# Last stage: GpSimd folds eight expert products to four only, TensorE sums four products and the tokens

## What is computed

```python
router_probs = softmax(x @ router_w + router_b)
top_p, top_i = top_k(router_probs, 2)
top_p = top_p / sum(top_p)
expert_out = einsum('bnd,edc->bnec', x, expert_w) + expert_b
return einsum('bnk,bnkc->bnc', top_p, take_along_axis(expert_out, top_i))
```

## Time and profile before

| what | us |
|---|---|
| median of 3 runs | 2697.78 |
| lowest and highest run | 2696.98, 2702.96 |
| the profiled execution, its own time | 2704.11 |
| its span in the profile | 2702.3 |
| PE, DVE, ACT, POOL busy in the span | 2410.5, 2324.5, 1593.5, 408.6 |

### The profile page before, as it was taken

One profiled execution on the slowest core, in us unless ns is written; L12 is line 12 of the kernel. 1 busy time (PEld: TensorE's weight loads), 2 busy tenths in 40 slices (PEclk: granted clock), 3 DMA queues, 4 the chain that ended last, 5 costly groups with the idle time before them and its releaser, 6 DMA issues. The chain is left out here.

```text
span 2702.3 us, 46968 instructions
## 1 busy us (share of the span) xinstructions
PE 2410.5 (89%) x18454; PEld 973.5 (36%) x18454; DVE 2324.5 (86%) x4150; ACT 1593.5 (59%) x2090; POOL 408.6 (15%) x456
## 2 busy tenths in 40 slices
PE   3878888369999999999999999999999998898886
PEld 1343333112222222222222222222222224787875
DVE  4577776689999999999999999999999992889997
ACT  1243343427777777777777777777777775343333
POOL 0021111300000000100000000000000000466666
PEclk9989899659999999999999999999999998667777
DMA  7696684320202222012022022021020001132231
GB/s 171 162 250 202 198 253 139 142 78 1 61 1 61 53 75 61 27 35 61 1 61 60 1 61 61 1 60 40 22 61 4 22 25 54 67 108 86 95 108 24
DMA packets 68110, 206.29 MB, mean 76 GB/s; under 512 B 20630, under 2 KB 33554, under 8 KB 61234
## 3 DMA queue, kind: packets, MB, share of 16 engines
q1 hardware_dynamic: 64034, 185.27, 24.7%
q0 software_dynamic: 3040, 15.57, 1.5%
q10 hardware_dynamic: 816, 2.46, 0.3%
HBM read 80.14 MB, written 61.31 MB: 52 GB/s over the span
## 5 line engine op out<-in xcount | busy, mean ns | idle before, releaser
L1331 DVE TENSOR_REDUCE at_XM<-at_psX 128x1 f32<-128x448 f32 x2688 | 1546.1, 620 | 92.0 <-PE at_psX L1182 71.2
L1248 ACT ACTIVATE at_PR<-at_psS 128x896 f32<-128x896 f32 x1344 | 1163.1, 915 | 454.4 <-PE at_psS L1158 452.4
L1200 PE MATMUL at_psV<-at_PR,at_V 128*32 128x448 f32 x5376 | 645.2, 552 | 0.1
L1158 PE MATMUL at_psS<-at_US,at_KS 128*128 128x448 f16 x2688 | 637.0, 357 | 0.7 <-ACT at_PR L1248 0.2
L1182 PE MATMUL at_psX<-at_KS,at_US 64*128 64x448 f16 x1344 | 490.5, 365 | 65.0 <-DVE at_XM L1331 42.7
L1182 PE MATMUL at_psX<-at_KS,at_UH 64*128 64x448 f16 x1344 | 490.5, 365 | 0.0
L1182 PEld LDWEIGHTS at_psX<-at_KS,at_US 64*128 64x128 f16 x1344 | 124.6, 93 | 721.5 <-DVE at_XM L1331 662.0
L1158 PEld LDWEIGHTS at_psS<-at_US,at_KS 128*128 128x128 f16 x2688 | 200.9, 98 | 273.8 <-ACT at_PR L1248 117.1
L1297 POOL CAST at_mrow<-at_mt 7x128 f16<-7x128 f32 x64 | 18.0, 281 | 1612.9 <-DVE at_mt L1350 1260.1
L1602 POOL TENSOR_TENSOR fi_WE<-fi_WE 128x256 f32<-128x256 f32 (+1 forms) x224 | 214.8, 984 | 101.5 <-DVE fi_WE L1656 101.1
L1465 PE MATMUL fi_psO<-fi_wv,fi_SUMS 128*128 128x33 f32 x800 | 153.0, 364 | 6.4 <-PEq L951 6.4
(11 more groups left out here) (199 smaller groups left out, 2010.0 us busy)
## 6 DMA issues: line engine op xcount, KB each, us to landing
sums<-at_O SPq DMA_DIRECT2D x16, 1568.0 KB, 6.3
fi_SUMS<-sums SPq DMA_DIRECT2D x16, 1568.0 KB, 6.8
sb_stacks<-sb_T SPq DMA_DIRECT2D x64, 270.5 KB, 7.3
sb_stacks<-sb_Xp SPq DMA_DIRECT2D x64, 248.8 KB, 10.2
sb_stacks<-sb_Xp SPq DMA_DIRECT2D x64, 248.0 KB, 5.9
sb_stacks<-sb_T SPq DMA_DIRECT2D x64, 172.5 KB, 11.4
at_KS<-key_stacks SPq DMA_DIRECT2D x32, 208.0 KB, 6.8
fi_RES<-residual SPq DMA_DIRECT2D x16, 400.0 KB, 7.2
```

The costliest lines, as they stand in the source:

```text
L1158: last = nc.tensor.matmul(psS[:, at % 2, k, 0:TILE], KS[:, b, (2 * c + k) * P:(2 * c + k + 1) * P], US[:, b, t * TILE:(t + 1) * TILE], sta ...
L1200: last = nc.tensor.matmul(psV[C * q:C * q + C, 0:TILE], V[:, b, G * k + q, :], PR[:, (n * 2 * STEPS + 2 * q4 + q // 2) % PRS, q % 2, :], s ...
L1248: nc.scalar.activation(PR[:, f % PRS], psS[:, at % 2, :, 0:TILE], ACT.Exp).then_inc(p_ready, 1)
L1331: nc.vector.tensor_reduce(o, psX[:, (at + j) % 3, 0:TILE], AX.X, ALU.max).then_inc(x_done, 1)
```

## The change

GpSimd makes only the first fold of each set, from eight products to four, and signals `folded` after it; the second fold, and the wait on its own first one, are gone. TensorE adds four products and the tokens per set, five products instead of three.

```diff
 def sums(n, c):
-                    for e in range(E // 4 + 1):
-                        v = (WE[:, s, e] if e < E // 4 else T1[:, c, G * s:G * s + w // C]).rearrange("p q c -> p (q c)")
+                    for e in range(E // 2 + 1):
+                        v = (WE[:, s, e] if e < E // 2 else T1[:, c, G * s:G * s + w // C]).rearrange("p q c -> p (q c)")
                         last = nc.tensor.matmul(psB[0:w, s // 4, s % 4 * P:(s % 4 + 1) * P], v[:, 0:w], ident[:],
-                                                start=(e == 0), stop=(e == E // 4))
+                                                start=(e == 0), stop=(e == E // 2))
                     last.then_inc(set_done, 1)
...
                 if n > 0:
-                    for s in range(QSETS + 1):
-                        if s < QSETS:
-                            pool.wait_ge(we_ready, n * NU - NU + min(2 * s + 2, NU))
-                            fold(s, E // 2).then_inc(half_folded, 1)
-                        if s >= 1:
-                            pool.wait_ge(half_folded, n * QSETS - QSETS + s)
-                            fold(s - 1, E // 4).then_inc(folded, 1)
+                    for s in range(QSETS):
+                        pool.wait_ge(we_ready, n * NU - NU + min(2 * s + 2, NU))
+                        fold(s, E // 2).then_inc(folded, 1)
```

More of the change, by code:

```diff
@@ L1406, in finish @@
         names = ("o_full o_done t1_ready t1_cen t1_sq t1_var t1_std xh_ready z_high z16_ready k_full zs_ready "
-                 "l_full lg_ready gap_ready gap_exp gates_ready e_full we_ready half_folded folded set_done out_ready order")
+                 "l_full lg_ready gap_ready gap_exp gates_ready e_full we_ready folded set_done out_ready order")
         (o_full, o_done, t1_ready, t1_cen, t1_sq, t1_var, t1_std, xh_ready, z_high, z16_ready, k_full, zs_ready,
-         l_full, lg_ready, gap_ready, gap_exp, gates_ready, e_full, we_ready, half_folded, folded, set_done, out_ready,
+         l_full, lg_ready, gap_ready, gap_exp, gates_ready, e_full, we_ready, folded, set_done, out_ready,
          order) = map(sem, names.split())
```

## The result

The kernel with the change takes **2717.99 us** (median of 4 runs, 2716.81 to 2720.4) where the kernel before took 2697.38 beside it (4 runs, 2694.81 to 2702.96): a ratio of **1.0065 [1.0049, 1.0082]**, 13 to 22 us slower. The forecast was 8.6 slower. The direction held. The range, 2697 to 2718, held by 0.01 us, and that is luck: more than half of the loss was not in the sum.

What follows compares the result with a forecast made beforehand. VectorE was taken to lead from `lsum`, with GpSimd's folds only disturbing it. A cycle of 9.04 + 10.05 + 5.9 = 24.99 against 24.59 gives 5.6 over 14; the end brings 8.6, on 2697.78: 2706.4 us, range 2697 to 2718.

Steps and rivals of the forecast that it cites:

- Part 1, fourteen more products: In `sums` on TensorE: products at 0.2235 us each delay unit 2, so `lsum` follows after 9.04 us instead of 7.61.
- The sign named beforehand: Transposes to next `sums`: the forecast is wrong if this stretch moves from 5.9 us by more than 0.3.
- Part 2, the relief: VectorE from `lsum` to transposes: without second folds L1690 and L1702 save 0.76 us together, giving 10.05 us.
- no relief for VectorE: Rival, `lsum` to transposes: L1690 and L1702 stay slow, cycle 25.75 us, total 2717; chance 0.13.
- That L1700 gains nothing: VectorE's L1700, 1.69 us: partly under a first fold that stays, so no gain was taken there.
- TensorE leads from `lsum` to transposes: Rival: with TensorE's 0.66 us slack gone, it costs 0.5 us per cycle in the mean, total 2713.4; chance 0.13.
- The clock stays up: Rival: TensorE's clock holds through project, transposes to `sums` some 0.8 us shorter, total 2694.3; chance 0.12.
- Part 3, the end: After the last `sums` starts: TensorE leads instead of GpSimd, four products at 0.45 us; 3.0 us later.
- The bound with all products slow: At the end of the span: every product of the last `sums` at 0.45 us, about 9 us later.

Runs made afterwards that it cites:

- e10: The change plus one spare, unread product on TensorE ahead of the last transpose; 2709.28 us, 1.0039 against the kernel before.
- e1: The changed kernel with TensorE back at three products per set, two remaining products left out of the sum; 2687.01 us, 0.9953 against the kernel before.
- e2: The kernel before with all second folds kept and TensorE adding five products per set, two counted twice; 2721.11 us, 1.0072.
- e5: The kernel before with sets 0 and 1 folded once and set 2's first fold held until VectorE made Z; 2679.71 us, 0.9924.
- e4: The change plus two spare, unread products on TensorE, ahead of the last transpose and of units 0 and 1; 2709.55 us, 1.0032 against the kernel before.
- e9: The change run once more, unaltered; 2717.59 us, 1.0067 against the kernel before.
- e11: The change plus one spare, unread product on TensorE ahead of units 0 and 1 only; 2717.03 us, 1.0065 against the kernel before.

## Why the prediction was right in direction and short in size

- **Part 1, fourteen more products.** Right wherever the clock was at 1.00: `lsum` 9.04 us behind `sums`, unit 2 after 8.0 (forecast 9.04 and 7.92), the idle time before unit 2 gone. **This is the term that was mis-sized**: it priced every product of the loop at 0.2235 us. In 5 of 15 cycles `sums` began at 0.50, took 9.1 to 9.5 us instead of 8.07, and pushed `lsum` to 10.06 to 10.41. With the longer way from the transposes (6.52) that is 7.3 us in 14 cycles, and nothing in the sum stood for it. The sign named beforehand, a stretch from transposes to `sums` off 5.9 by more than 0.3, is there in just these cycles. The kernel before had shown the rise at least 1.1 us ahead of `sums` each time, and I took that for granted in a kernel whose cycle was to be another length. No rival stood for it either. e10 shows the forecast with this one thing mended: 1.0039, some 11 us (6 to 15), cycle 25.06, end 28.77 (forecast 24.99 and 28.6).
- **Part 2, the relief.** Right: 180 and 375 ns in all images, `lsum` to transposes 10.00 (forecast 10.05), and e1 and e2 show it from both sides. The rival *no relief for VectorE* gave 2717, next to the measured 2718, but for a cause that did not occur: its cycle of 25.75 needs 540 and 778 ns. The range's upper end, 2718, had been set above this rival, so it covered the measured time by a case that did not happen. A total that fits is not a mechanism; e2 is the kernel that it describes. That L1700 gains nothing was right for this change, since the first fold of set 2 stays, and e5 shows the 0.70 us that lay there.
- **TensorE leads from `lsum` to transposes**: no. The way is 10.00 in every cycle, and the transposes start right behind VectorE's copy.
- **The clock stays up**: no. It did hold longer, falling 2.4 to 5.8 us behind `lsum` where it was 0.6 ahead of it to 3.0 behind before, but it fell in every cycle. Two stretches of the changed kernel, in the columns of the windows above, show the clock at 1.00 with TensorE busy 2.27 of 2.40 us, and at 0.50 right behind with 9.98 of 10.00 busy:

```profile
2462.80:2465.20 2.40, 2.27 (x22) 2.14 (x21) 2.37 (x4) 0.41 (x1) 0.00 (x0) 1.00 0.00 0
2465.40:2475.40 10.00, 9.98 (x56) 8.69 (x57) 9.40 (x20) 5.32 (x9) 3.80 (x3) 0.50 0.54 169
```

  The Trainium skill, page TensorE: Matmul & The Clock Gate (Why this matters for your kernels), puts the fall down to idle gaps between bursts. This trace again shows a fall without such a gap, so the rule would have led to the wrong forecast here. For the rise the runs go both ways: one product in place of 0.26 us of idle time brought it ahead of `sums` in all cycles of e4 and e10, but in the stretch at 9.98 of 10.00 busy it did not come.
- **Part 3, the end.** Forecast 3.0, measured 5.3. The mechanism was right (TensorE leads in place of GpSimd), the count of slow products was not: ten, not four, which is 1.1 us; and the fifteenth `sums` began at half clock, which brought the last one 1.1 us later than forecast. (The bound with all products slow, put at about 9, comes to 9.8 by its own terms.)
- **The whole.** 5.6 for the cycles as forecast, 7.3 for late rises, 5.3 at the end and 0.2 at the start make the 18.2 of the profiled stage, to the rounding; the medians, 20.6 apart, agree within their interval.

## What to carry to other kernels

Before moving work off an engine, find out which instructions of it hold another engine (shortest against median duration of single lines, beside the timeline), and move only those: here two second folds of seven held VectorE; without these two, and with one first fold delayed, the ratio was 0.9924; without all seven, TensorE adding four products in every set for it, 1.0065. Work moved to an engine is free only as far as the idle time that it fills, so count what fits. Where the matrix engine's clock changes inside each cycle, price every added product at both levels, and check how close the rise lies to the dense part, because a change of the cycle's length can move it, as I read these runs.

## What the runs showed of the hardware

- A fold on GpSimd doesn't slow VectorE in proportion; it stops it. L1690 ended 0.03 us after the folds above it did, at 540 ns instead of 180; the copy took 778 instead of 375 and ended 0.24 us after its folds, the subtraction 1.69 us instead of 0.98. It does not hold every instruction: the reduction L1689, which ran from 2467.16 to 2468.13 under the same two folds as L1690, took 972 ns, and its shortest run is 970. It works the other way too: the pair of folds over the subtraction took 2.71 us, another pair 1.95. The Trainium skill, page SBUF — State Buffer (SBUF: two separate sides), describes a pair of ports that VectorE and GpSimd share as an exclusive lock, held for a whole instruction; the trace agrees.
- A single float32 product of 0.44 us (0.74 at half clock), ahead of one transpose, kept the rise of the clock at least 0.5 us ahead of `sums` in 30 cycles (e4, e10), where it came 2 to 3 behind in 15 of 45 without it (the change, e9, e11), and made a kernel with more work 8 us faster. I had not expected so short a gap to matter.
